# Projections of a fused attention and expert kernel: ten piece buffers, finer waits, mixed job order, and row fills by transfers

## The reference

```python
x = x + _L0_xattn_ref(_layernorm(x), ctx, Wq, Wkv, Wout, bout)
#   q = x @ Wq;  k, v = split(concat(mem, x) @ Wkv);  dots = q k^T * d**-0.5
#   mask j > i + mem_len;  softmax(dots) @ v;  @ Wout + bout
x = x + _L0_ffn_ref(_layernorm(x), Wg, W1, W2)
#   probs = softmax(x @ Wg); each expert takes its top T/E tokens;
#   out += gate * gelu(x @ W1[e]) @ W2[e]
```

## Time and profile before

| | us |
|---|---|
| median of 3 runs (505.65 to 510.08) | 507.42 |
| the profiled execution, its own time | 509.3 |
| its span, first to last instruction | 507.5 |
| projections, start to first score matmul | 113.7 |
| attention | 205.3 |
| output projection and routing | 81.0 |
| experts | 107.5 |

### The profile page before, as it was taken

One profiled execution on the slowest core, in us unless ns is written; L12 is line 12 of the kernel. 1 busy time (PEld: TensorE's weight loads), 2 busy tenths in 40 slices (PEclk: granted clock), 3 DMA queues, 4 the chain that ended last, 5 costly groups with the idle time before them and its releaser, 6 DMA issues.

```text
span 507.5 us, 8833 instructions
## 1 busy us (share of the span) xinstructions
PE 391.2 (77%) x2753; PEld 229.3 (45%) x2756; DVE 234.8 (46%) x858; ACT 262.1 (52%) x361; POOL 104.9 (21%) x154
## 2 busy tenths in 40 slices
PE   0386984479999997999799998889511689989994
PEld 0332741263332422332233332767400688878883
DVE  6967782422343523443343443888688830011111
ACT  1133342238999895999589997322400025444440
POOL 8513850410000000000000000000000033555552
PEclk9999899698999997999899999999655599999998
DMA  8004572387040404040404700024200021222220
GB/s 281 3 31 133 160 219 86 104 275 255 3 135 4 135 1 134 0 134 1 135 0 120 223 2 1 0 84 163 87 1 0 1 57 51 85 68 80 68 64 31
DMA packets 30254, 43.32 MB, mean 85 GB/s; under 512 B 5166, under 2 KB 18096, under 8 KB 30208
## 3 DMA queue, kind: packets, MB, share of 16 engines
q1 hardware_dynamic: 27536, 36.17, 22.5%
q0 software_dynamic: 2672, 6.61, 4.3%
HBM read 30.76 MB, written 13.58 MB: 87 GB/s over the span
## 4 chain that ended last, share of the span: by engine, by line
PE 52%; DVE 22%; ACT 11%; issue 10%; DMA 3%; POOL 1%; DVEq 1%; POOLq 0%; ACTq 0%; SPq 0%
PE ps L828 17%; PE ps L812 10%; ACT pbuf L667 9%; PE ps L987 7%; PE ps L997 7%; PE ps L784 3%; DVE pbuf L1066 3%; DVE v_st L1292 3%; PE ps L913 2%; DMA k_cut<-piece 1%; DVE pbuf L1158 1%; DVE n L1125 1%; DVE nt L1063 1%; PE ps L929 1%; PE ps L793 1%
## 5 line engine op out<-in xcount | busy, mean ns | idle before, releaser
L667 ACT ACTIVATE pbuf<-ps 128x1024 f32<-128x1024 f32 (+3 forms) x192 | 173.2, 990 | 28.9 <-PE ps L812 28.9
L1202 DVE SCALAR_TENSOR_TENSOR pbuf<-pbuf,seen 128x128 f32<-128x128 f32 (+2 forms) x288 | 68.1, 275 | 104.7 <-ACT pbuf L667 104.7
L812 PE MATMUL ps<-q_st,k_st 98*128 98x512 bf16 (+4 forms) x512 | 99.4, 326 | 13.9 <-ACT pbuf L667 11.2
L828 PE MATMUL ps<-pbuf,v_st 128*32 128x512 f32 (+4 forms) x1024 | 91.6, 487 | 7.0 <-DVE mid L1208 5.5
L812 PEld LDWEIGHTS ps<-q_st,k_st 98*128 98x128 bf16 x512 | 39.6, 99 | 83.1 <-ACT pbuf L667 45.3
L828 PEld LDWEIGHTS ps<-pbuf,v_st 128*32 128x32 f32 x1024 | 27.1, 110 | 56.2 <-issue 32.0
L1393 DVE SCALAR_TENSOR_TENSOR mid<-ps,slot_gate,mid 128x256 f32<-128x256 f32 x20 | 9.7, 484 | 81.3 <-PE ps L997 81.3
L704 ACT COPY piece<-wts 128x1024 f32 x20 | 20.9, 1047 | 48.4 <-DVE more L1380 45.1
L997 PE MATMUL ps<-wts,mid 128*128 x160 | 38.9, 387 | 5.1 <-ACT mid L714 3.4
L987 PE MATMUL ps<-mid,piece 128*128 128x128 f32 x320 | 39.1, 275 | 1.2 <-issue 1.2
L987 PEld LDWEIGHTS ps<-mid,piece 128*128 128x128 f32 x320 | 38.7, 192 | 2.6 <-issue 1.7
(11 more groups left out here) (203 smaller groups left out, 450.8 us busy)
## 6 DMA issues: line engine op xcount, KB each, us to landing
wts<-in_L_ffn_W SPq DMA_DIRECT2D x16, 512.0 KB, 8.5
k_st<-k_cut SPq DMA_DIRECT2D x48, 147.2 KB, 2.9
q_st<-q_cut SPq DMA_DIRECT2D x48, 128.0 KB, 2.7
token_rows<-pbuf SPq DMA_DIRECT2D x4, 1024.0 KB, 4.3
q_cut<-piece SPq DMA_DIRECT2D x8, 384.0 KB, 2.6
k_cut<-piece SPq DMA_DIRECT2D x8, 384.0 KB, 3.0
xres<-in_x SPq DMA_DIRECT2D x4, 512.0 KB, 6.4
pbuf<-in_L_xattn_Wkv SPq DMA_DIRECT2D x1, 512.0 KB, 7.2
```

The costliest lines, as they stand in the source:

```text
L667: nc.scalar.activation(pbuf[:, s % 2, r, c0:c1], st_ps[(s * GH + r) % NST][:, c0:c1], ACT.Exp, scale=SCALE).then_inc(exp_done, 1)
L812: last = nc.tensor.matmul(st_ps[(s * GH + r) % NST][:, a:z], k_st[pa][:, r, t * P:(t + 1) * P], q_st[pa][:, r, q0 + a - c0:q0 + z - c0], s ...
L828: last = nc.tensor.matmul(o_ps[32 * r:32 * r + 32, a:z], v_st[pa][:, t, r, :], pbuf[:, s % 2, r, a + dc:z + dc], start=(t == 0), stop=(t = ...
L1202: last = nc.vector.scalar_tensor_tensor(a, a, 3.0e38, seen[:, off:off + w], ALU.min, ALU.mult)
```

## The change

It gives the projection stage ten piece buffers (in the space that W1 takes later) and three remainders; mixes the job order, so that the first q job comes after the context and half of the flips, v jobs lie between q and k jobs, and each batch gets a head-sum job "n"; makes a flip wait for each row tile and a q, k or v job only for the flips that it reads; uses all eight banks. The square is now made on ScalarE from the high part in SBUF, one job later, together with the cast to the middle part (`middle`), which leaves DVE. DVE takes the maximum of the squares of each feature row in SBUF; the norm matmuls are gone, and so are POOL's reductions over partitions: the peaks are summed over the 16 features of a head by the four small matmuls of job "n", and DVE multiplies and compares. That bound sums peaks of features, where the old one took the peak of sums, and SAFE is 70. The two-row fills are transfers issued by ScalarE, which also issues the context's loads. DVE's constants are cut into five parts (`DURING`). The bias adds come behind the last piece on POOL, and DVE waits for them at `take_outputs`. SP stages the first buffer pair after five stores, and loads W1 in three lots behind the first group and later stagings, with W2's early part after them.

```diff
-NPIECES = 3
+NPIECES = 10
+NREM = 3
...
-SAFE = 40.0
+SAFE = 70.0
...
-piece_f = sb("piece", [P, NPIECES * 3 * 512 // 2])
-piece = piece_f[:, :].bitcast(BF16).rearrange("p (a c n) -> p a c n", a=NPIECES, c=3)
+piece = w1_sb[:, 0:NPIECES * 3 * 512 // 2].bitcast(BF16).rearrange("p (a c n) -> p a c n", a=NPIECES, c=3)
+piece_f = sb("piece_f", [P, 2304])
...
 def jobs_of(b):
-    jobs = [("t", b, q4, k) for q4 in range(2) for k in range(KT)] + [("c", b)]
-    for m in range(KT):
-        jobs += [("q", b, m, n0, 512) for n0 in range(0, S, 512)]
-        jobs += [("k", b, m, n0, min(512, J - n0)) for n0 in range(0, J, 512)]
-    return jobs + [("v", b, t) for t in range(0, JT, 2)]
+    q = [[("q", b, m, n0, 512) for n0 in range(0, S, 512)] for m in range(KT)]
+    k = [[("k", b, m, n0, min(512, J - n0)) for n0 in range(0, J, 512)] for m in range(KT)]
+    v = [("v", b, t) for t in range(0, JT, 2)]
+    flip = [[("t", b, q4, c) for c in range(KT)] for q4 in range(2)]
+    jobs = [("c", b)] + flip[0] + [q[0][0], v[0], k[0][0], v[1]] + flip[1]
+    if b == 0:
+        return jobs + [q[0][1], k[0][1], k[0][2], q[1][0], v[2], q[1][1], v[3], k[1][0], v[4], k[1][1], k[1][2]]
+    return (jobs + [("n", 0), q[0][1], k[0][1], k[0][2], q[1][0], v[2], q[1][1], k[1][0], k[1][1], k[1][2], v[3], v[4]]
+            + [("n", 1)])
 JOBS = jobs_of(0) + jobs_of(1)
-NBK = 7
+NBK = 8
...
-    store_pieces(0, PER_B)
-    sp.wait_ge(ones_rows, 2)
...
+    store_pieces(0, PER_HALF)
     for i in range(NPIECES):
-        sp.wait_ge(qk_out[i], 16 * stores(i, PER_B))
-    for pa in range(2):
-        stage(pa, 0, 0)
+        sp.wait_ge(qk_out[i], 16 * stores(i, PER_HALF))
+    stage(0, 0, 0)
+    store_pieces(PER_HALF, PER_B)
+    stage(1, 0, 0)
     store_pieces(PER_B, 2 * PER_B)
-    for e in range(E):
-        sp.dma_start(w1_sb[:, e * KT * F:(e + 1) * KT * F].rearrange("p (k n) -> p k n", k=KT),
-                     W1[e].rearrange("(k p) n -> p k n", p=P)).then_inc(w1_in, 16)
-        if e < E_EARLY:
-            sp.dma_start(w2_sb[:, e * FT * D:(e + 1) * FT * D].rearrange("p (k n) -> p k n", k=FT),
-                         W2[e].rearrange("(k p) n -> p k n", p=P)).then_inc(w2_in, 16)
     for i in range(NPIECES):
...
+    sp.wait_ge(lo_done, len(QK))
     shift_rows(0, 0)
-    with sp.Fori(0, NG - 1) as it:
+    first_weights(range(0, 3))
+    for it in range(NG - 1):
         shift_rows(1, it * 2 + 1)
         sp.wait_ge(pv_done, it * (2 * NSTEP) + NSTEP + 2)
         stage(0, (it + 1) // 2, (it + 1) % 2)
+        if it < 2:
+            first_weights(range(3 + 3 * it, min(6 + 3 * it, E)))
+        else:
+            second_weights(range(0, E_EARLY))
...
-    pool.dma_start(ctx_sb[:, :, 0, :], ctx[:, 0:P, :].rearrange("b p d -> p b d")).then_inc(ctx_in, 16)
-    pool.dma_start(ctx_sb[0:M - P, :, 1, :], ctx[:, P:M, :].rearrange("b p d -> p b d")).then_inc(ctx_in, 16)
+    nc.gpsimd.memset(ones_b[:, :], 1.0).then_inc(ones_made, 1)
+    nc.gpsimd.memset(zeros_b[:, :], 0.0).then_inc(ones_made, 1)
...
-        pool.wait_ge(st_made, made)
-    for i in range(2):
-        nc.gpsimd.memset(q_st[i][KROWS:SROWS, :, :].rearrange("p h n -> p (h n)").bitcast(F32), 0.0).then_inc(st_made, 1)
-        made += 1
-        pool.wait_ge(st_made, made)
-        nc.gpsimd.memset(k_st[i][KROWS:SROWS, :, 0:J], 1.0).then_inc(ones_rows, 1)
-        pool.wait_ge(ones_rows, i + 1)
+    pool.wait_ge(st_made, made)
     for i in range(2):
         nc.gpsimd.memset(v_st[i][:, 0:JT - 1, :, HD:HD + 1], 1.0).then_inc(st_made, 1)
         made += 1
...
-        if i == PER_B:
-            pool.wait_ge(bias_in, 16)
-            pool.wait_ge(xn_done, TT)
-            for t in range(TT):
-                nc.gpsimd.tensor_tensor(xres[:, t, :], xres[:, t, :], bias, ALU.add).then_inc(biased, 1)
+        if i == PER_B + 1:
             pool.wait_ge(vcopy_done, len(VJ) // 2)
             for pa in range(2):
                 load_v(pa, 0, 0)
         pool.wait_ge(mid_done, i + 1)
-        nc.gpsimd.tensor_tensor(piece[:, i % NPIECES, 2, 0:w], rem[:, i % 2, 0:w],
+        nc.gpsimd.tensor_tensor(piece[:, i % NPIECES, 2, 0:w], rem[:, i % NREM, 0:w],
                                 piece[:, i % NPIECES, 1, 0:w], ALU.subtract).then_inc(low_done, 1)
-        if i == PER_B + 2:
-            over_partitions(0)
-    over_partitions(1)
+    pool.wait_ge(bias_in, 16)
+    pool.wait_ge(xn_done, TT)
+    for t in range(TT):
+        nc.gpsimd.tensor_tensor(xres[:, t, :], xres[:, t, :], bias, ALU.add).then_inc(biased, 1)
...
+    act.dma_start(ctx_sb[:, :, 0, :], ctx[:, 0:P, :].rearrange("b p d -> p b d")).then_inc(ctx_in, 16)
+    act.dma_start(ctx_sb[0:M - P, :, 1, :], ctx[:, P:M, :].rearrange("b p d -> p b d")).then_inc(ctx_in, 16)
+    act.wait_ge(ones_made, 2)
+    for i in range(2):
+        act.dma_start(k_st[i][KROWS:SROWS, :, :].rearrange("p h n -> p (h n)").rearrange("p (a n) -> p a n", n=P),
+                      ones_b[0:SROWS - KROWS, None, :].broadcast_to([SROWS - KROWS, GH * JP // P, P])).then_inc(ones_rows, 16)
+        act.dma_start(q_st[i][KROWS:SROWS, :, :].rearrange("p h n -> p (h n)").rearrange("p (a n) -> p a n", n=P),
+                      zeros_b[0:SROWS - KROWS, None, :].broadcast_to([SROWS - KROWS, GH * S // P, P])).then_inc(ones_rows, 16)
     root(0)
-    root(1)
-    nqk = 0
+    nqk = nt = 0
+    part_due = None
+    def middle(i):
+        w = JOBS[QK[i]][4]
+        act.wait_ge(hi_done, i + 1)
+        if i >= NREM:
+            act.wait_ge(norm_done, i - NREM + 1)
+        nc.scalar.activation(sq[:, i % NREM, 0:w], piece[:, i % NPIECES, 0, 0:w], ACT.Square).then_inc(sq_done, 1)
+        act.wait_ge(lo_done, i + 1)
+        nc.scalar.copy(piece[:, i % NPIECES, 1, 0:w], rem[:, i % NREM, 0:w]).then_inc(mid_done, 1)
...
+        if job[0] == "n":
+            continue
         act.wait_ge(proj_ready, jn + 1)
...
             if nqk >= NPIECES:
                 act.wait_ge(qk_out[sl], 16 * (nqk // NPIECES))
             nc.scalar.copy(piece[:, sl, 0, 0:w], bk[:, 0:w]).then_inc(hi_done, 1)
-            if nqk >= 2:
-                act.wait_ge(norm_ready, nqk - 1)
-            nc.scalar.activation(sq[:, nqk % 2, 0:w], bk[:, 0:w], ACT.Square).then_inc(sq_done, 1)
+        if part_due is not None:
+            middle(part_due)
+            part_due = None
+        if job[0] in "qk":
+            part_due = nqk
             nqk += 1
+            if nqk == 3:
+                root(2)
+            if nqk == 6:
+                root(3)
+                nc.scalar.activation(warm[:, :], rstd[0:1, 0:1], ACT.Exp)
...
-    nc.scalar.activation(warm[:, :], rstd[0:1, 0:1], ACT.Exp)
...
-    def norms(i):
-        w = JOBS[QK[i]][4]
-        pe.wait_ge(sq_done, i + 1)
-        if i >= 1:
-            pe.wait_ge(norm_done, i)
-        nc.tensor.matmul(bank(7)[:, 0:w], heads[:, :], sq[:, i % 2, 0:w], start=True, stop=True).then_inc(norm_ready, 1)
-    normed = 0
...
-            if jn == 0:
-                pe.wait_ge(ident_made, 2)
-            pe.wait_ge(xn_done, b * QT + 4 * q4 + 4)
             for i in range(4):
+                pe.wait_ge(xn_done, b * QT + 4 * q4 + i + 1)
                 last = nc.tensor.transpose(bk[:, i * P:(i + 1) * P],
                                            xn[:, b * QT + 4 * q4 + i, k * P:(k + 1) * P], ident[:, :])
...
+        elif job[0] == "n":
+            pe.wait_ge(heads_made, 1)
+            pe.wait_ge(bound_done, 2 * KT * (b + 1))
+            for m in range(KT):
+                for c in range(2):
+                    at = (c * KT + m) * P
+                    last = nc.tensor.matmul(bk[0:1, at:at + P], bpeak[:, b, m, c:c + 1], heads[:, :], start=True, stop=True)
...
             pe.wait_ge(w_in, 32)
-            pe.wait_ge(tr_done, len(TR) // 2 * (b + 1))
+            pe.wait_ge(tr_done, flipped(b, c0 + w))
...
-        while normed < len(QK) and QK[normed] <= jn - 2:
-            if normed == 0:
-                pe.wait_ge(heads_made, 1)
-            norms(normed)
-            normed += 1
-    pe.wait_ge(vcopy_done, len(VJ))
-    pe.wait_ge(lo_done, len(QK))
-    pe.wait_ge(norm_done, len(QK))
+    for jn in range(len(JOBS) - NBK, len(JOBS) - 2):
+        free_bank(jn)
     pe.wait_ge(low_done, len(QK))
+    pe.wait_ge(ones_rows, 16 * 4)
...
+            for jn in range(len(JOBS) - 2, len(JOBS)):
+                free_bank(jn)
...
     stats_in(0)
+    rows_in(0)
     stats_in(1)
-    rows_in(0)
     rows_in(1)
-    v.wait_ge(iota_made, 5)
     def indices(op, val):
...
             o = b * PER_B + m * PER_HALF
-            seq(nc.vector.reduce_max(bnd[:, 0:1], n2[:, o:o + 2], AX.X))
-            seq(nc.vector.reduce_max(bnd[:, 1:2], n2[:, o + 2:o + PER_HALF], AX.X))
-            seq(nc.vector.tensor_tensor(bnd[:, 2 + m:3 + m], bnd[:, 0:1], bnd[:, 1:2], ALU.mult))
-        nc.vector.tensor_tensor(bmax[:, b:b + 1], bnd[:, 2:3], bnd[:, 3:4], ALU.max).then_inc(bound_done, 1)
+            for c, (a, z) in enumerate([(o, o + 2), (o + 2, o + PER_HALF)]):
```

(41 more changed lines are left out.)

98 lines of the change are left out of this document (57 added, 41 removed).

## The result

The changed kernel takes 496.04 us (median of four runs, 494.79 to 496.84) against 507.02 for the kernel before (505.65 to 510.08): ratio 0.976, 95% interval 0.973 to 0.980. It is faster by some 11 us where 37 were forecast, and lies above the range.

The account below looks back on a forecast made before the run. The prediction took the time to the first score matmul as what the change could shorten, with DVE last: 113.7 to 74.8, 38.9 us, less 1 for masks and 0.5 for PE's clock, 37.4; 507.4 - 37.4 = 470.0 us, range 461 to 482.

Parts of the forecast that it names:

- Square from SBUF, middle cast on ScalarE: Projection stage: ScalarE's 9 us of added casts make 43 us within 60 and cost nothing while outside DVE's loop.
- PE's eight banks absorb this: Projection stage: DVE's last piece at 70.8 us, behind PE's last k job at 63.4, would not hold PE up.
- PE's line: Projection stage: jobs summed from 12.4 us at 1.72 per wide job, last v job ending at 66.8 without waits.
- The second rival: Projection stage: ScalarE and DVE wait for each other piece by piece, 9 us later, 479 us; chance 0.2.
- DVE's line decides: Projection stage: DVE, not PE, is last, its last bound at 71.5 us; first score at 74.8 instead of 113.69.
- The start: Kernel start: with fills by transfers, the first projection begins at 12.4 us instead of 26.09, bounds 11.5 and 15.
- Ten buffers: Projection stage: ScalarE's 31.0 us of waits for stores go, with 8 us of cover behind staging.
- Constants: Projection stage, DVE's line: expert 4.2, order 2.0 and digit constants 2.0 us, set between the later pieces.
- The masks and bias adds: First attention group: POOL's 16 adds run from 72 to 83 us beside some 4 masks, costing 1 us.
- the third rival: First attention group: masks locked out by POOL's adds, 4 us, 473 us, only from first score before 76; chance 0.06.
- the flag stays 0: Attention branch: the new bound, 43,380 and 45,057, stays below 78,400, so the shift branch stays unused; costs nothing.
- the weights' later loading: Attention: weights queued behind staging sets on SP are free; up to 7 us in one group if cover is gone.

Follow-up runs that it names:

- j_load: b_cast plus one cast per piece on ScalarE that nobody reads and that waits for nothing of DVE's; 487.5 us, ratio 0.964.
- b_cast: Changed kernel with the middle cast of the remainder back on DVE, ScalarE only squaring; 484.0 us, ratio 0.955.
- c_const: Changed kernel with DVE's expert, order and digit constants moved behind the last piece; 484.9 us, ratio 0.955.
- g_comb: Changed kernel with the edits of b_cast and c_const together; 479.8 us, ratio 0.948.
- k_fills: g_comb with ScalarE's four row-fill issues moved behind the work of the first rows; 475.6 us, ratio 0.943.
- i_fill: Changed kernel with the two-row strips filled by POOL again instead of by transfers; 502.4 us, one run.
- f_late: Changed kernel with ScalarE's cast of a remainder one job later, behind the next copy; 492.3 us, ratio 0.976.
- m_three: g_comb with three piece buffers instead of ten, and the two waits this needs; 489.4 us, ratio 0.969.
- a_defer: Changed kernel with DVE making the next remainder before it takes the maximum of the last square; 496.0 us, ratio 0.977.
- d_loop: Changed kernel with all early weights loaded before the attention loop and SP's group loop a machine loop again; 495.2 us, ratio 0.979.
- e_three: Changed kernel with three piece buffers instead of ten; 500.0 us, ratio 0.985.
- h_early: Changed kernel with the second batch's statistics ahead of the first piece and its row normalisations behind pieces 0 and 1; 492.3 us, ratio 0.975.

## Why the prediction was wrong, by its own steps

**The step that failed** is "*Square from SBUF, middle cast on ScalarE* … Nothing, while it isn't in DVE's loop", and with it "PE's eight banks absorb this". Its argument was a sum: 43 us of ScalarE within 60. The sum was right (41.8 measured), the conclusion was not, for two reasons that the runs part. First, the cast waits for a remainder whose place in DVE's program is behind blocks of 2 to 3 us, and ScalarE, which works its program in order, holds back every later copy: 15.2 us of waits. The Trainium skill (PSUM — Partial Sum Buffer, "Engine vs sequencer instructions") says that the queues of ScalarE, VectorE and GpSimd are strict first in, first out; the trace agrees: between 32.2 and 35.39 no copy passed the waiting cast, although PE had finished the next q job at 32.06 and a v job at 33.80. Second, the added work by itself is not free: up to 5.7 us by j_load, with ScalarE busy 46% of the time. Both delay the copies of the second batch's flipped rows, for which free banks are no help, because PE needs those rows; and the banks did not suffice either, since PE had waited 1.96 us for one before that batch's second flip job. Of the 19.8 us by which the first score missed, 12.9 were there at the second batch's first projection. The second half of PE's line took 29.3 us instead of 25.3 (two jobs slow behind the pause, 3.75 and 2.74, where the line had 1.72 and 1.73; another pause of 0.94), and from PE's last projection to the first score 10.9 instead of 8.0.

**The second rival** had this mechanism (the square after the next copy, a late remainder holding the cast) and was given 0.2, and 9 us: a handover of 0.5 us per piece. The casts' move costs more (10.0 us by b_cast, 12.8 between c_const and g_comb), and not evenly: it comes in lumps where DVE has a block. What a page of busy times can't show is which instruction stands ahead of which; the prediction wrote out DVE's line in order, ScalarE's only as a sum.

**"DVE's line decides"**: true at the end (the head sums waited 6.65 us for DVE) but late by 18.7 us (90.2 for 71.5), since DVE itself waited 29 us for ScalarE. Its durations were near: the maximum of a square from SBUF took 0.68 to 0.69 us (taken 0.68), digits 2.1 (2.0), expert constants 3.5 (4.2), head constants 2.3 (1.8), a bound 0.34 (0.7), the reading of the flag 1.5 (0.9). In g_comb the first score stands at 77.3, within 2.5 us of the 74.8, but that is partly luck: there DVE has the 20 casts more and 8 us of constants less than the forecast's line. With the cast alone (b_cast) it is 84.60, and PE's last projection ends at 72.8, not 66.8.

**The start**: 13.82 for 12.4. The term that was off is the issues: 7.7 us until ScalarE was free where 3.6 to 6 was the bound, because of the one of 3.50 us. With it out of the way, in k_fills, the first projection starts at 12.21. The fills were right: DVE's two long rows went, worth 7.1 us by i_fill.

**Ten buffers**: right that the waits of 31.0 us go and that none comes behind staging; but they covered other lateness, and only 5.6 us came through, 15.0 once the casts and the constants were out of the way.

**Constants**: placed in DVE's line at 8.2 us together; moving them away gave 4.6 us at the first score, 7.3 with the cast.

**The masks and bias adds**: the third rival had a mask locked out while POOL adds; the term itself went by the idle time between masks, 1 us. The traces side with the rival's mechanism. The adds and the first masks of the changed kernel:

```profile
90.40 10.95 POOL L582 TENSOR_TENSOR xres<-xres,mid 128x256 f32<-128x256 f32 x16
...
100.43 2.20 DVE L1234 SCALAR_TENSOR_TENSOR pbuf<-pbuf,seen 128x128 f32<-128x128 f32 x6 [6.59 <-ACT pbuf L709]
```

and the same six masks, with the shortest, the median and the longest in ns:

```profile
L1234 DVE SCALAR_TENSOR_TENSOR pbuf<-pbuf,seen x6: 277/281/1061, 100.4 to 102.3; 128x128 f32<-128x128 f32 x6
```

The first mask starts at 100.43 and takes 1.06 us, until 101.49, just after the last add ends at 101.35; the others take 0.28, as in the kernel before (0.29). In f_late a mask starts at 97.81 and takes 2.08 us, through almost three adds (0.69 apart), until 99.89; the adds end at 99.74. The same holds in all nine kernels in which a mask meets the adds: it ends 0.14 to 0.16 us behind the last one. In five of them it had started 0.9 to 1.9 us ahead of that end, more than one add lasts, so it is held until all of them are done and not for one. It cost little only because attention started late: one mask met them, for 0.78 us more, within the 1 us taken, and f_late's first group, with 1.8 us more, is as long as the kernel before's (27.7 us). The third rival needed a first score before 76, and no run tests it: in k_fills (76.19) and g_comb the first masks come at 84.47 and 85.73, behind the adds (82.61 and 83.87), since DVE is busy with the late constants until then (the digits take 3.8 us beside the adds, 2.1 without).

**Attention longer by 6.1 us** was not foreseen. 2.2 of it lie in the first group (29.8 us against 27.7 before): the granted clock was 0.84 there against 0.94 (0.50 over its first 5.9 us), and the first sixteen value matmuls took 3.64 us, the later ones 1.75 to 1.92. The forecast had 0.5 us for that. PE had waited 6.65 and 2.38 us just before; but b_cast, with 7.41 and 2.54, has 27.7 us for the group, so the waits alone don't decide it. Another 3.5 lie in the two passes of the loop's boundary. The timeline of PE, after, at both:

```profile
178.54 3.64 PE L869 MATMUL ps<-pbuf,v_st 128*32 128x512 f32 x16 [4.18 <-DVE mid L1241]
...
233.06 3.64 PE L869 MATMUL ps<-pbuf,v_st 128*32 128x512 f32 x16 [4.78 <-DVE mid L1241]
```

and DVE's, the copies it waits for:

```profile
177.19 1.22 DVE L1241 COPY mid<-ps 128x1024 f32 x1 [7.09 <-issue]
...
231.71 1.23 DVE L1241 COPY mid<-ps 128x1024 f32 x1 [7.69 <-issue]
```

Before, PE idles 2.68 and 2.80 us there, and DVE's idle time is 5.59 and 5.70. In b_cast, c_const, g_comb, j_load, k_fills and m_three PE idles 2.5 to 3.6 us, in a_defer, d_loop, e_three, f_late, h_early and i_fill 3.9 to 4.6, much as in the changed kernel (4.18 and 4.78). The engine that comes late is DVE, and it waits for nothing that the profile shows. All six quick kernels have DVE's program ahead of the loop in another form than the changed kernel, but so have a_defer and h_early; d_loop leaves little for staging and weights. The Trainium skill (Runtime: NRT & Kernel Launch, "Instruction fetch mechanics") says that a taken branch to a page that is not held waits for the fetch of that page; in the changed kernel's trace one instruction transfer of 0.01 MB lies in each of the stretches 171 to 174.4, 174.4 to 176.5 and 176.5 to 178.6, and around b_cast's boundary, whose gap is 2.60, there are three too. That decides nothing. Nor can it be only where the loop's code lies: c_const has the changed kernel's instructions, in another order ahead of the loop, and its gaps are 3.26 and 2.56. The cause stays open. The shorter attention, 5.1 us, and the 4.6 at the first score are most of what c_const gained in the median.

Right without more: the flag stays 0, PE's pitch of a job (1.72 us), the weights' later loading (d_loop, which undoes it, has a first score and attention 1.1 and 1.8 us shorter, no more than unrelated edits have).

## What to carry to other kernels

When work moves to an engine with time to spare, write out both engines' programs in order, each wait with what stands ahead of it on the other side and what is queued behind it on this one; a sum of busy times says nothing of either. In this kernel a short step (0.43 us) that needs another engine's result of the same piece was better kept on that engine, though that engine was the fuller one. Waits that vanish are worth only what was not late anyway: 31 us of them gave 5.6 here and 15.0 once the next lateness was gone. And a mean over a merged row can hide the one instruction that was held: six masks in 2.20 us are one of 1.06 and five of 0.28.

## What the runs showed of the hardware that was not expected

- Of six transfer issues in a row on ScalarE five took 0.52 to 0.81 us and the last 3.50 (2.99 to 3.67 in the other kernels that issue six); in k_fills the two at 12 us took 0.81 and 0.64, the two at 16 us 0.63 each.
- A mask on DVE (two inputs in SBUF) that starts beside POOL's adds ends about 0.15 us after the last of them, in f_late through almost three in a row: 1.06 us in the changed kernel and 2.08 in f_late, for 0.28. POOL's two-row fills held DVE's four-element instructions in the same way (4.09 and 0.98 us for 0.17 in i_fill).
- A pause of 7 us on TensorE cost more than itself: the granted clock fell to 0.56 over the 9.4 us stretch in which PE worked 1.12, and the job behind it took 3.75 us for 1.88; behind a pause of 1.9 us (b_cast, 46.63) it took 1.96.
- The idle time of PE at the boundary of the same attention loop was 2.5 to 3.6 us in six kernels and 3.9 to 4.8 in seven, by edits that touch no instruction of the loop's work on PE, DVE or ScalarE.
